# V for two heads at once, four steps to a pair of heads, and an attention written out without loops

## The reference

```python
q = (x @ wq.T).reshape(Bx, Tx, N_HEADS, D_HEAD).transpose(0, 2, 1, 3)
k = (x @ wk.T) ...   # the same
v = (x @ wv.T) ...   # the same
q = rmsnorm(q, q_norm_w)
k = rmsnorm(k, k_norm_w)
q = apply_rope(q, rope_cos, rope_sin)
k = apply_rope(k, rope_cos, rope_sin)
scores = jnp.einsum('bhtd,bhsd->bhts', q, k) * scale
scores = LOGIT_SOFTCAP * jnp.tanh(scores / LOGIT_SOFTCAP)
scores = jnp.where(mask[None, None], -jnp.inf, scores)
attn = jax.nn.softmax(scores, axis=-1)
out = jnp.einsum('bhts,bhsd->bhtd', attn, v)
out = out.transpose(0, 2, 1, 3).reshape(Bx, Tx, N_HEADS * D_HEAD)
return out @ wo.T
```

## Time and profile before

| | |
|---|---|
| three runs, median | 1119.45 us (1116.04 to 1123.36) |
| the profiled execution, its time | 1122.51 us |
| the profiled execution, its span | 1120.8 us |
| mean granted TensorE clock | 0.964 |
| busy: PE, DVE, ACT, POOL | 1038.1, 831.9, 699.9, 631.6 us |

### The profile page before, as it was taken

One profiled execution on the slowest core, in us unless ns is written; L12 is line 12 of the kernel. 1 busy time (PEld: TensorE's weight loads), 2 busy tenths in 40 slices (PEclk: granted clock), 3 DMA queues, 4 the chain that ended last, 5 costly groups with the idle time before them and its releaser, 6 DMA issues.

```text
span 1120.8 us, 20581 instructions
## 1 busy us (share of the span) xinstructions
PE 1038.1 (93%) x6304; PEld 831.9 (74%) x6304; DVE 831.9 (74%) x1360; ACT 699.9 (62%) x1159; POOL 631.6 (56%) x668
## 2 busy tenths in 40 slices
PE   4688999999999999999999999999999959989766
PEld 3567888888888888888888888888888746445432
DVE  3377888888888888888888898988898775713203
ACT  3465777777777777777777777777777632322212
POOL 0265666666666666666666666666666652363332
PEclk9899999999999999999999999999999887989977
DMA  9100000000011010101000000000000009539427
GB/s 331 31 29 30 29 29 28 28 28 28 28 33 40 30 38 20 37 24 33 25 32 28 28 28 28 28 28 28 28 28 20 20 3 294 138 96 268 74 29 229
DMA packets 47195, 65.99 MB, mean 59 GB/s; under 512 B 7904, under 2 KB 38592, under 8 KB 47168
## 3 DMA queue, kind: packets, MB, share of 16 engines
q1 hardware_dynamic: 43376, 60.65, 17.6%
q0 software_dynamic: 3072, 4.46, 2.2%
q10 hardware_dynamic: 720, 0.54, 0.2%
HBM read 54.35 MB, written 11.29 MB: 59 GB/s over the span
## 4 chain that ended last, share of the span: by engine, by line
PE 78%; DMA 11%; DVE 5%; issue 2%; POOL 2%; ACT 1%; SPq 1%; ACTq 0%; POOLq 0%; DVEq 0%
PE ps L387 20%; PE ps L388 19%; PE ps L389 19%; PE ps L415 9%; DMA acc_rows<-ye,acci 7%; PE ps L421 4%; PE ps L559 2%; PE ps L603 2%; DMA qsq<-rq_rows 1%; DMA yacc<-in_x 1%; DVE prob_lo L1057 1%; POOL pacc L933 1%; PE ps L569 1%; DVE qhat_lo L1057 1%; POOL xg L1013 1%
## 5 line engine op out<-in xcount | busy, mean ns | idle before, releaser
L1057 DVE TENSOR_TENSOR prob_lo<-praw,prob_hi 128x1024 fp32r<-128x1024 f32 (+7 forms) x256 | 313.2, 1251 | 3.2 <-ACT prob_hi L718 3.2
L916 POOL TENSOR_SCALAR_AFFINE_SELECT praw<-praw 128x128 f32<-128x128 f32 x256 | 119.6, 469 | 307.0 <-ACT praw L765 288.4
L933 POOL TENSOR_TENSOR pacc<-pacc,praw 128x768 f32<-128x768 f32 (+2 forms) x192 | 241.8, 1259 | 16.6
L759 ACT ACTIVATE praw<-ps,rk 128x1024 f32<-128x1024 f32 (+7 forms) x256 | 186.0, 740 | 88.3 <-PE ps L389 78.5
L718 ACT ACTIVATE prob_hi<-praw 128x1024 fp32r<-128x1024 f32 (+7 forms) x256 | 168.0, 683 | 1.1 <-POOL praw L916 1.1
L765 ACT ACTIVATE praw<-praw 128x1024 f32<-128x1024 f32 (+7 forms) x256 | 167.4, 681 | 0.0
L387 PE MATMUL ps<-qhat_hi,kT_hi 128*128 128x512 f32 (+3 forms) x384 | 136.4, 355 | 13.4 <-DVE qhat_lo L1057 12.9
L387 PE MATMUL ps<-prob_hi,vS_hi 128*128 128x512 f32 (+3 forms) x384 | 136.1, 354 | 4.0 <-DVE prob_lo L1057 4.0
L389 PE MATMUL ps<-qhat_hi,kT_lo 128*128 128x512 f32 (+3 forms) x384 | 133.9, 349 | 0.0
L388 PE MATMUL ps<-qhat_lo,kT_hi 128*128 128x512 f32 (+3 forms) x384 | 133.9, 349 | 0.0
L388 PE MATMUL ps<-prob_lo,vS_hi 128*128 128x512 f32 (+3 forms) x384 | 133.3, 347 | 0.0
(11 more groups left out here) (155 smaller groups left out, 1961.1 us busy)
## 6 DMA issues: line engine op xcount, KB each, us to landing
qsq<-rq_rows SPq DMA_DIRECT2D x32, 512.0 KB, 3.7
wgu<-in_wgu SPq DMA_DIRECT2D x16, 704.0 KB
wd<-in_wd SPq DMA_DIRECT2D x16, 352.0 KB
wraw<-in_wqkv SPq DMA_DIRECT2D x16, 256.0 KB, 3.7
acc_rows<-pacc SPq DMA_DIRECT2D x8, 512.0 KB, 10.9
wv<-in_wqkv SPq DMA_DIRECT2D x16, 128.0 KB, 2.1
woraw<-in_wo SPq DMA_DIRECT2D x16, 128.0 KB, 2.0
yacc<-in_x SPq DMA_DIRECT2D x1, 2048.0 KB, 14.0
```

The source lines that it names most:

```text
L759: nc.scalar.activation(praw[:, raw_at(b, j)], buf[:, P * j:T], ACT.Tanh, scale=rk[:, b, j:j + 1]).then_inc(tanh_done, 1)
L916: nc.gpsimd.affine_select(out=diag, in_=diag, compare_op=ALU.is_ge, fill=0.0, base=0, pattern=[[1, P]], channel_multiplier=-1).then_inc(ma ...
L933: nc.gpsimd.tensor_tensor(pacc[:, P * j:T], before, raw, ALU.add).then_inc(pacc_done, 1)
L1057: v.tensor_tensor(dst, x_, hi.bitcast(F32), ALU.subtract).then_inc(done, 1)
```

## The change

- The 32 steps are ordered by pairs of heads: head 2p batch 0, head 2p+1 batch 0, head 2p batch 1, head 2p+1 batch 1. These are the four steps q = 0 to 3 of a pair; k = q % 2 is the head within the pair.
- V is made for both heads of a pair at once, by `mm3`: `xT` against a `wv` of 256 columns that is split into a high and a low part by DVE (`split_values_weights`, in step 3 of a pair). A unit is two tiles of tokens, 12 matmuls of 256 columns. A batch has four units for two heads: vd (tiles 0 and 1) in the odd step before, va and vb (2, 3 and 4, 5) in the even step, vc (6 and 7) in the odd step. vc stands ahead of k0, the others late in the step.
- On DVE, q's split stands right behind its scaling, ahead of tile 3 and of the V unit's low part; turn_rms stands ahead of tile 0 instead of behind it. The split of `wo` stands at the start of the steps 0 and 1 of a pair, the split of the next `wqk` in the steps 2 and 3.
- The weights of two heads are loaded at a time, each kind behind one of the broadcasts. Before the first step there are more loads: `wqk`, `wv` and `wo` of two heads instead of one.
- The steps are written out on every engine; there is no loop.

The core of the diff:

```diff
-UNIT_ORDER = "q0 q1 k0 k1 ss sums op0 op1 v0 op2 op3 v1".split()
+EVEN = "q0 q1 k0 k1 ss sums op0 op1 va op2 op3 vb".split()
+ODD = "q0 q1 vc k0 k1 ss sums op0 op1 op2 op3 vd".split()
 BEHIND = {"sums", "op0", "op1", "op2", "op3"}
-PROLOGUE = "q0 q1 k0 k1 v0 v1 ss".split()
+PROLOGUE = "q0 q1 k0 k1 vd ss".split()
+V_TILES = {"vd": 0, "va": 1, "vb": 2, "vc": 3}
...
-                    for j in range(4):
-                        t0 = b * T + 512 * half + P * j
+                    for i in range(2):
+                        t0 = b * T + P * (2 * V_TILES[what] + i)
                         for c in range(KC):
-                            last = mm(bank[:, P * j:P * j + P], xraw[:, c, t0:t0 + P], wv[:, c, :], start=c == 0, stop=c == KC - 1)
+                            last = mm3(bank[:, 2 * DH * i:2 * DH * i + 2 * DH], of(xT, ALL, c, slice(t0, t0 + P)), of(wv, ALL, c, ALL),
+                                       c == 0, c == KC - 1)
...
+            for p in range(0, NP_ - 1):
+                sp.wait_ge(wvlo_done, p + 1)
+                for e in range(2):
+                    sp.dma_start(wvraw[:, e], ...).then_inc(wv_in, 16)
+                rq_broadcast(p * STEPS + 1, 1)
+                sp.wait_ge(wlo_done, p * 2 + 2)
+                for e in range(2):
+                    sp.dma_start(wraw[:, e], ...).then_inc(w_in[e], 16)
+                rq_broadcast(p * STEPS + 2, 0)
+                sp.wait_ge(wolo_done, p * 2 + 2)
+                for e in range(2):
+                    sp.dma_start(woraw[:, e], ...).then_inc(wo_in[e], 16)
+                rq_broadcast(p * STEPS + 3, 1)
+                rq_broadcast(p * STEPS + 4, 0)
...
# PE, in a step
+                scores(s, k, 0)
+                if k:
+                    project("vc", k, st.b, *st.unit("vc"))
                 if new:
+                    project("k0", 1 - k, st.next_b, *st.unit("k0"))
...
+                scores(s, k, 5)
+                if not k:
+                    project("va", k, st.b, *st.unit("va"))
+                if old:
+                    out_proj(s - 1, 1 - k, 2, *st.unit("op2"))
+                values(s, k, 0)
+                if old:
+                    out_proj(s - 1, 1 - k, 3, *st.unit("op3"))
+                if not k:
+                    project("vb", k, st.b, *st.unit("vb"))
+                values(s, k, 1)
+                if k and new:
+                    if st.q == 3:
+                        pe.wait_ge(wvlo_done, st.pair + 2)
+                    project("vd", k, 1 - st.b, *st.unit("vd"))
+                scores(s, k, 6)
+                scores(s, k, 7)
+                values(s, k, 2)
...
# DVE, in a step
+                if st.q < 2:
+                    split_output_weights(st)
...
+                    if st.b and not st.last:
+                        split_next_weights(st.pair + 1, k, st.unit("q0")[0] - 1)
+                if old:
+                    summed(1 - k, *st.unit("sums"))
+                    out_projected(st.old_b, 1 - k, 0, s - 1, *st.unit("op0"))
                 if new:
                     turn_rms(s + 1)
+                tile(s, k, 0)
+                if old:
+                    out_projected(st.old_b, 1 - k, 1, s - 1, *st.unit("op1"))
+                tile(s, k, 1)
+                if not k:
+                    values_in("va", st.group("va"), *st.unit("va"))
+                elif st.q == 3 and new:
+                    split_values_weights(st.pair + 1, st.unit("vc")[0])
+                if old:
+                    out_projected(st.old_b, 1 - k, 2, s - 1, *st.unit("op2"))
+                tile(s, k, 2)
+                if old:
+                    out_projected(st.old_b, 1 - k, 3, s - 1, *st.unit("op3"))
                 if new:
+                    if st.q == 3:
+                        dve.wait_ge(gcur_done, st.pair + 2)
+                    scale_raw(s + 1, 1 - k)
+                    split_queries(s + 1, 1 - k)
+                tile(s, k, 3)
+                if not k:
+                    values_in("vb", st.group("vb"), *st.unit("vb"))
+                elif new:
+                    values_in("vd", st.group("vd"), *st.unit("vd"))
```

More of the change, by code:

```diff
@@ L529, in step @@
-                if new:
-                    project("v1", 1 - b, *hd.unit(b, "v1"))
-                values(s, b, 1)
-                scores(s, b, 6)
-                scores(s, b, 7)
-                values(s, b, 2)
-            first, last = Head(0, "first"), Head(H - 1, "last")
-            step(first, 0, old=False)
-            step(first, 1)
-            with pe.Fori(1, H - 1) as h:
-                for b in range(B):
-                    step(Head(h, "middle"), b)
-            step(last, 0)
@@ L543, in _ @@
-            step(last, 1, new=False)
-            end, s = Head(H, "tail"), B * H
+                    out_proj(s - 1, 1 - k, 3, *st.unit("op3"))
[8 more added lines that the diff above has]
+                scores(s, k, 7)
@@ L546, in _ @@
+                values(s, k, 2)
+            for q in range(STEPS):
+                step(Step(0, q, "first"))
+            for p in range(1, NP_ - 1):
+                for q in range(STEPS):
+                    step(Step(p, q, "middle"))
+            for q in range(STEPS):
+                step(Step(NP_ - 1, q, "last"))
+            end, s = Step(NP_, 0, "tail"), B * H
             for j in range(3, TT):
                 values(s - 1, 1, j)
-            sums(s - 1, 1, *end.unit(0, "sums"))
+            sums(s - 1, 1, *end.unit("sums"))
@@ L960, in step @@
-                mask(s, b, 5)
-            first, last = Head(0, "first"), Head(H - 1, "last")
-            pool.wait_ge(zeros_out, 16 * ((2 * ACCR // P * D + T - 1) // T + 1))
-            step(first, 0, old=False)
-            step(first, 1)
-            with pool.Fori(1, H - 1) as h:
-                for b in range(B):
-                    step(Head(h, "middle"), b)
-            step(last, 0)
-            step(last, 1, new=False)
+                    rms_keys(1 - k)
+                mask(s, k, 4)
@@ L972, in _ @@
+                mask(s, k, 5)
+            pool.wait_ge(zeros_out, 16 * ((2 * ACCR // P * D + T - 1) // T + 1))
+            for q in range(STEPS):
+                step(Step(0, q, "first"))
+            for p in range(1, NP_ - 1):
+                for q in range(STEPS):
+                    step(Step(p, q, "middle"))
+            for q in range(STEPS):
+                step(Step(NP_ - 1, q, "last"))
             for j in (6, 7):
```

424 lines of the change are left out of this document (210 added, 214 removed).

## The result

The changed kernel takes 1144.33 us (median of four, 1139.1 to 1149.06) where the kernel before, run beside it, takes 1120.38: a ratio of 1.0204, 95% interval 1.0168 to 1.0240. It is slower by 2%. The forecast was 1127, in a range of 1097 to 1146. The profiled execution took 1145.42 us, with a span of 1143.7 and a mean granted clock of 0.962.

A forecast was written before the change was run, and what follows sets the result against it. PE bounded the kernel before; after the change a mark-to-mark loop through DVE and the transfer would, 110.0 us a pair of heads against 107.84. With ramp and tail that is +8 us: 1127 us, range 1097 to 1146.

The forecast's parts named there:

- The stop at the mark: PE waits at the mark (q1's first matmul) for DVE's vS_lo: 1.4 us behind step 1, 2 us behind step 3.
- PE's own share: PE's work in a step falls from 26.96 to 26.21 us with the new V units, 24 us in all.
- The restart: PE restarting after a wait at the mark: 0.1 us in step 0.
- The transfer: turn_rms to scaling, through DRAM and the broadcast back: 6.2 us, taken from 6.52 and 5.90.
- wo: Split of wo at the start of step 0 meets POOL's additions: 1.3 us; in step 1 it should fit in.
- vc: V unit ahead of k0 on PE in odd steps: what follows on PE stands 1.42 us later after the mark.
- second rival: Collisions feed on themselves: a late mark puts wo behind POOL; a pair 3.4 us longer, 1151 us; chance 0.22.
- Ramp and tail: Ramp, steps 0 to 2: mark of step 2 at 93 us, gain 6.9; tail, last step: +0.4 us.
- The loops: Writing out the loops on every engine gives 0, with bounds of 0 and 0.5 us a step.
- rival 3: Fetch of the written-out code stalls some engine, 0.5 us a step: 1143 us; chance 0.06.
- PE stays the bound: First rival: each of the 28 steps takes PE's 26.21 us, -28 us, 1092 us; chance 0.17.
- The collisions: The second rival: late marks put the split of wo beside POOL's additions, +24 us, 1151 us; chance 0.22.

The follow-up runs named there:

- a_old_order: Changed kernel with the split of q put back behind tile 3 and the V low part: 1121.17 us.
- b_split_first: Kernel before with only the split of q moved right behind its scaling: 1143.49 us, ratio 1.0208.
- a_old_wo_turn: Changed kernel with q's split behind tile 3 and the V low part, wo's split behind the sums of squares, turn_rms ahead of op0: 1106.56 us.
- a_wo_behind_ss: Changed kernel with the split of wo behind the fold of the sums of squares: 1140.83 us.
- four cases of vc: Changed kernel 1144.3 us; with vc cut to 4 of 12 matmuls 1143.2; with vc's copy-out ahead of tile 5 on DVE 1142.9; with both 1124.5.
- a_turn_late: Changed kernel with turn_rms behind tile 0 again: 1192.18 us.
- b_no_loops: Kernel before with its five loops written out, nothing else: 1125.80 us, ratio 1.0044.
- a_vb_short: Changed kernel with the V unit vb cut to 4 of its 12 matmuls: 1141.66 us.

## Why the prediction was right in its mechanism and 17 us short

**The stop at the mark: right.** The forecast was that DVE's vS_lo would stop PE at the mark since 2.0 us of split stand ahead of it, much behind odd steps and hardly behind even. The waits show this and nearly nothing else, and a_old_order and b_split_first show the cause from both sides. Scaling to mark was put at 4.7 and is 4.74. Mark to turn_rms was put at 16.72 in step 1 and is 17.00 (287.59 to 304.59); in step 3 it was put at 16.97 and is 17.39 (231.96 to 249.35). In step 3 the scaling was to be late and not waiting for DMA: so it is in five of seven pairs (255.91 is one), and in step 2, for which this was not forecast, in most too. The first whole pair of heads, marks from 150.15 to 260.65, took 110.5 us, forecast 110.0; the mean of the six pairs up to 820.81 is 111.8. The time, 1144.33, lies 2 us inside the end of the range, 1146, and the forecast change of 8 us is a third of the measured one. That the range held is partly luck: three terms below were too small and one was left out, and wo, which was too large, made up for a part.

**PE's own share: too small.** I had 26.21 us a step. A step that ends without a stop takes 231.96 - 205.51 = 26.45, with 0.11 in it of the restart at 205.51; in a_old_wo_turn, where neither end has a stop, it is 26.34 (279.30 to 305.64). The new V unit is 1.44 where I had 1.42, and the output projection behind it still takes 0.76 us at 223.31 (0.79 behind an old unit, 0.71 at 225.45, where no V unit is in front); I had nothing for that. So a step saves 0.62 and not 0.75, and the whole change had 20 us to gain at most, not 24.

**The restart: too small.** I took 0.1 us for a PE that restarts; it is 0.27 beside the bracket. Twenty stops make 5.4 us. There are 14 more halts that no line of the waits names, most of them twice in a pair of heads, in step 3: at k1 (239.55, 0.52 us behind the matmul before it instead of 0.23) and at the V unit vd (254.49). Each costs 0.35 to 0.39 us, 5.2 in all. At k1 it is DVE's low part of vc, which ends at 239.50; what ends those at vd is open.

**The transfer: too small.** From turn_rms to a scaling that waited for DMA it is 6.62 us at 276.15 and 6.92 at 304.59, and 6.1 to 7.3 in all 16, 6.69 in the mean; I took 6.2, the mean of two steps. The page gives 3.9 us from issue to landing for the broadcast, 3.7 before. What makes it longer is open. Step 9 (287.59 to 316.27), in the place of the forecast's step 1, took 28.68 us for 27.6.

**wo: too large in effect.** The split of wo does meet POOL's additions, in steps 0 and 1 alike (I had step 1 free): 1.86 us for a mean wo_lo, 0.51 before. But of the 1.3 us that I put on PE in step 0 hardly any arrives: step 8 (260.65 to 287.59) takes 26.94 us for 27.6, and the 3.5 us of a_wo_behind_ss are within the noise.

**vc: right in size, wrong in cause.** I had the odd loop 1.42 us longer and put it down to PE's vc alone. The four cases of vc show DVE's queue beside it, of the same length. Whoever had shortened vc by this sum would have gained nothing.

**The clock: not in the sum.** I had it only in the second rival. Behind three of the stops the granted clock falls. Matmuls of q1 are 0.23 us apart behind the first one at 287.59 and 0.43 behind the stop of 2.09 us:

```profile
316.73 0.63 PE L418 MATMUL ps<-xT_lo,wqk_hi 128*128 128x512 f32 x1
317.16 0.63 PE L419 MATMUL ps<-xT_hi,wqk_lo 128*128 128x512 f32 x1
...
319.91 0.40 PE L418 MATMUL ps<-prob_lo,vS_hi 128*128 128x512 f32 x1
320.14 0.39 PE L419 MATMUL ps<-prob_hi,vS_lo 128*128 128x512 f32 x1
```

That is nearly a factor of two, so the lower of the clock's two levels (1.2 GHz for 2.4), for some 3.6 us, and the step then takes 28.05 instead of 26.45. In the view by stretches:

```profile
316.00:344.00 28.00, 27.73 (x167) 23.57 (x168) 23.01 (x34) 19.55 (x32) 16.95 (x16) 0.94 0.06 20
```

Three such stretches (from 316, 484 and 541 us) have a granted clock of 0.94 where the others have 1.00, 4.8 us in all. In a_turn_late there are 11, and it lost 48 us where 28 x 1.1 is 31.

**Ramp and tail.** The mark of step 2 came at 94.83, forecast 93. The mark of step 30 came at 876.47, forecast 863. Behind it 267.2 us follow, forecast 266.5.

**The loops: wrong.** Forecast 0, measured 5 us, 2 to 8 by the interval (b_no_loops); rival 3 had 16 with a chance of 0.06.

**The rivals.** PE stays the bound (1092) is out: 90% busy on the page is less than before, with less work. The collisions (1151) came near in size and had the wrong place: the stops at the mark lengthen by transfer (0.5 us and not 2.1), restart and clock, and hardly by wo. The account of the 28 steps, 27.90 against PE's 26.34, is 43.7 us: stops 26.3, restarts 5.4, two stops at the q copy 1.8, clock 4.8, the 14 unnamed halts 5.2; 0.2 us are left over.

## What to carry to other kernels

Count a saving on the busiest engine only up to the next path's slack: here 1.6 us of slack in a loop through DVE, POOL and DRAM, and 2.0 us put into it cost more than the 20 us that V could give. An operation is moved for free only if nothing that another engine waits for stands behind it; in b_split_first that one move, two lines, cost 23 us. When cutting something on the path gains nothing, look at the next wait of the same engine before saying that it was off the path: two ways of equal length look like none.

## What the runs showed of the hardware

A stop of PE costs 0.27 us more than its bracket, as the end of a matmul is modelled 0.16 us past the start of the next, and the first matmul behind a stop keeps the next for 0.34 instead of 0.23 us.

The length of a stop alone does not decide whether the clock falls. In the changed kernel, from 100 to 880 us, it stayed up behind all stops up to 2.01 us (at 709.04) and fell behind those of 2.09, 2.12 and 2.47. But in a_turn_late it stayed up behind a stop of 3.04 us (802.97, above), and in a_vb_short it fell behind one of 1.79:

```profile
313.24 0.50 PE L417 MATMUL ps<-xT_hi,wqk_hi 128*128 128x512 f32 x1 [1.79 <-DVE vS_lo L1102]
...
314.74 0.63 PE L419 MATMUL ps<-xT_hi,wqk_lo 128*128 128x512 f32 x1
```

That matmul takes 0.63 us, as those behind 316.27 in the changed kernel, for 0.39 at the full clock.

Operations of DVE whose inputs all lie in SBUF are stretched by POOL's additions, those with an input in PSUM are not. wo_lo took 2.22 us at 260.83, and POOL's first addition ran from 260.54 for 2.23:

```profile
260.54 2.23 POOL L976 TENSOR_TENSOR pacc<-praw 128x896 f32<-128x896 f32 x1 [0.15 <-POOL pacc L972]
...
262.92 1.85 POOL L976 TENSOR_TENSOR pacc<-pacc,praw 128x768 f32<-128x768 f32 x1
```

The two q copies at 262.98, from PSUM, took 1.28 us beside the next addition, no longer than 0.68 each. From 100 to 880 us, 21 low parts of V (one input in PSUM, one in SBUF) began under an addition and took 0.68 us in the mean, 0.69 where none ran. The Trainium skill (SBUF — State Buffer, Who interferes with whom) says that a DVE instruction with two SBUF inputs contends with a GpSimd instruction that reads SBUF, that one with at most one SBUF input, outside the two-port modes, does not, and that issue order decides who blocks. The trace agrees: wo_lo starts 0.3 us behind the addition and ends 0.3 us behind it. POOL pays little: 2.23 for an addition that took 2.12 in the earlier trace rows.
